# One array shape for a recommendation tower: sums and full-width steps in array tiles of 64 rows by 32 columns, one bank of sums per target, chunks of 64 steps

## What is computed

```python
e = jnp.stack([tbl_0[ids[:, 0]], ..., tbl_31[ids[:, 31]]], axis=1)        # 2048 x 32 x 64
z = jnp.sum(e, axis=-1)
outer = jnp.einsum('bpd,pde,bpe->bp', e[:, II, :], kernels, e[:, JJ, :])  # 496 pairs
h = jnp.concatenate([z, outer, dense_ctx], axis=1)                        # 544 wide
h = jnp.maximum(h @ W_top1 + b_top1, 0.0)                                 # 512
h = jnp.maximum(h @ W_top2 + b_top2, 0.0)                                 # 256
y = h @ W_top3
```

## Time and profile before

| | |
|---|---|
| median of 3 runs | 868.84 us (868.46 to 869.98) |
| the profiled execution | 869.06 us, span 867.2 us |
| PE busy, matmul records | 842.1 us (97%), 6584 |
| PE weight loads, records | 403.7 us, 6584 |
| DVE busy | 622.6 us (72%) |
| POOL busy | 483.9 us (56%) |
| ACT busy | 151.9 us (18%) |
| granted TensorE clock | 1.00 throughout |

### The profile page before, as it was taken

One profiled execution on the slowest core, in us unless ns is written; L12 is line 12 of the kernel. 1 busy time (PEld: TensorE's weight loads), 2 busy tenths in 40 slices (PEclk: granted clock), 3 DMA queues, 4 the chain that ended last, 5 costly groups with the idle time before them and its releaser, 6 DMA issues.

```text
span 867.2 us, 15755 instructions
## 1 busy us (share of the span) xinstructions
PE 842.1 (97%) x6584; PEld 403.7 (47%) x6584; DVE 622.6 (72%) x706; ACT 151.9 (18%) x273; POOL 483.9 (56%) x518
## 2 busy tenths in 40 slices
PE   2999999999999999999999999999999999999998
PEld 1888888776645333333333333333333333333333
DVE  1776677688865888888855488888855678888850
ACT  1222312212311220120210320020111212011002
POOL 6765777777777777777776477667733430000000
PEclk9999999999999999999999999999999999999999
DMA  9511111111111111111111011111100000000000
GB/s 327 195 25 25 27 32 28 27 29 30 27 28 26 28 28 26 31 27 26 28 26 25 16 24 26 25 25 26 26 13 13 14 16 1 1 1 1 1 1 1
DMA packets 24353, 28.32 MB, mean 33 GB/s; under 512 B 13398, under 2 KB 13657, under 8 KB 24156
## 3 DMA queue, kind: packets, MB, share of 16 engines
q0 software_dynamic: 16384, 16.81, 9.8%
q1 hardware_dynamic: 7888, 10.49, 3.6%
q10 hardware_dynamic: 12, 0.01, 0.0%
HBM read 27.27 MB, written 0.01 MB: 31 GB/s over the span
## 4 chain that ended last, share of the span: by engine, by line
PE 95%; DVE 2%; DMA 1%; issue 1%; POOL 1%; ACT 0%; DVEq 0%; ACTq 0%
PE y L610 52%; PE acc L627 26%; PE y L657 5%; PE y L593 4%; PE y L685 3%; DVE prod L558 2%; PE y L668 2%; PE y L662 1%; PE y L698 1%; POOL rows L365 1%; DMA rows<-tbl,ids_sb 1%; PE y L639 0%; DMA ids_sb<-ids 0%; DVEq L259 0%; ACT h L478 0%
## 5 line engine op out<-in xcount | busy, mean ns | idle before, releaser
L558 DVE TENSOR_TENSOR prod<-y,xt 128x1024 f32<-128x1024 f32 (+2 forms) x600 | 581.8, 1031 | 198.3 <-PE y L610 197.3
L365 POOL DMA_INDIRECT rows<-tbl,ids_sb x512 | 483.2, 944 | 222.8 <-issue 112.1
L610 PE MATMUL y<-xt,kw 64*128 64x512 f32 (+2 forms) x2976 | 476.7, 462 | 4.7 <-DVE prod L558 3.5
L610 PEld LDWEIGHTS y<-xt,kw 64*128 64x128 f32 x2976 | 242.7, 189 | 219.3 <-issue 201.9
L627 PE MATMUL acc<-prod,ones_strip 128*32 128x512 f32 (+2 forms) x2976 | 239.4, 454 | 0.3 <-DVE prod L558 0.3
L627 PEld LDWEIGHTS acc<-prod,ones_strip 128*32 128x32 f32 x2976 | 79.4, 109 | 142.4 <-issue 68.1
L411 ACT COPY xt<-y 128x1024 f32<-128x1024 f32 (+3 forms) x56 | 36.2, 646 | 297.0 <-PE y L593 296.9
L593 PE MATMUL y<-ident,rows 128*128 128x128 f32 x256 | 41.2, 288 | 16.2 <-DMA rows<-tbl,ids_sb 16.1
L530 DVE TENSOR_REDUCE z_rows<-rows 128x8 f32<-128x512 f32 (+2 forms) x96 | 44.5, 497 | 15.0 <-DMA rows<-tbl,ids_sb 15.0
L442 ACT COPY h_in<-acc 128x512 f32<-128x512 f32 (+2 forms) x24 | 10.6, 443 | 240.4 <-PE acc L627 240.4
L593 PEld LDWEIGHTS y<-ident,rows 128*128 128x128 f32 x256 | 28.0, 142 | 40.8 <-issue 32.6
(11 more groups left out here) (23 smaller groups left out, 66.7 us busy)
## 6 DMA issues: line engine op xcount, KB each, us to landing
rows<-tbl,ids_sb POOLq DMA_INDIRECT x512, 2.4
kw<-pair_k SPq DMA_DIRECT2D x14, 512.0 KB, 11.4
w_sb<-w SPq DMA_DIRECT2D x1, 1024.0 KB
w_sb<-w SPq DMA_DIRECT2D x1, 512.0 KB
kw<-pair_k SPq DMA_DIRECT2D x1, 384.0 KB
kw<-pair_k SPq DMA_DIRECT2D x1, 256.0 KB, 3.9
w1z_sb<-w1z SPq DMA_DIRECT2D x1, 256.0 KB
ids_sb<-ids SPq DMA_DIRECT2D x1, 240.0 KB, 2.7
```

The source lines that it names most:

```text
L365: pool.indirect_dma_start(out=rows[:, s, c, h, :], out_offset=None, in_=tables[f], in_offset=bass.IndirectOffsetOnAxis(ap=ids_sb[:, b, f:f ...
L558: nc.vector.tensor_tensor(prod_part(t, d, n), y_part(t, d, n), x, ALU.mult).then_inc(y_read, n)
L610: last = nc.tensor.matmul(y[:, h, :], kw[part, d, :], xt[part, slot_of(t, units[h][0] // 2), 0:w], start=True, stop=True)
```

## The change

All sums, and the steps of the tiles of 512 samples, are issued in array tiles of 64 rows by 32 columns. There are eight such tiles in the array: two halves of the rows by four quadrants of the columns.

- A step at width 512 issues eight matmuls in place of two: four column quadrants by two row halves, each 64 rows by 32 columns by 512. Steps at widths 128 and 256 keep their 64x128 matmuls.
- Each unit's sum issues two matmuls in place of one: partitions 0 to 63 (target n = 0) into bank 0 of `accs`, partitions 64 to 127 (n = 1) into bank 1. `ones_strip` has ones in one column. A quadrant has 32 places, so that a chunk is 64 steps (CHUNKS goes from 4 to 2).
- `accs` is one buffer of two banks where two buffers of one bank alternated. A chunk's first sum waits for ACT's copy of the chunk just before. ACT copies 128 x 1024 values in one instruction, half as often.
- `mlp1` reads four pieces as before: two of them before the last `acc_read` wait and two behind it, where it was three and one. The weights w1 are laid out to match.

```diff
-STRIPS = 16
+STRIPS = 32
+SPLIT_WIDTH = 512
+def step_columns(t):
+    return 32 if WIDTHS[t] >= SPLIT_WIDTH else P
 ...
-        accs = [bank(f"acc{i}", [P, TILE]) for i in range(2)]
+        accs = bank("accs", [P, 2, TILE])
 ...
-                nc.scalar.copy(h_in[:, c, 0:w], accs[(CHUNKS * t + c) % 2][:, 0:w]).then_inc(acc_read, 1)
+                nc.scalar.copy(h_in[:, c, :, 0:w], accs[:, :, 0:w]).then_inc(acc_read, 1)
 ...
-                for h in range(2):
-                    part = slice(DIM * h, DIM * h + DIM)
-                    last = nc.tensor.matmul(y[:, h, :], kw[part, d, :], xt[part, slot_of(t, units[h][0] // 2), 0:w],
-                                            start=True, stop=True)
+                size = step_columns(t)
+                for first in range(0, P, size):
+                    columns = slice(first, first + size)
+                    for h in range(2):
+                        part = slice(DIM * h, DIM * h + DIM)
+                        last = nc.tensor.matmul(y[columns, h, :], kw[part, d, columns],
+                                                xt[part, slot_of(t, units[h][0] // 2), 0:w], start=True, stop=True)
 ...
-                if first % CHUNK_STEPS == 0 and c >= 2:
-                    pe.wait_ge(acc_read, c - 1)
+                if first % CHUNK_STEPS == 0 and c >= 1:
+                    pe.wait_ge(acc_read, c)
                 pe.wait_ge(y_read, N_STEPS * t + end)
                 for u in range(2 * first, 2 * end):
                     q, s = unit_place(u)
-                    last = nc.tensor.matmul(acc[32 * q:32 * q + 32, 0:w], ones_strip[:, 30 - 2 * s:62 - 2 * s],
-                                            prod_part(t, u // 2)[:, u % 2, :],
-                                            start=s == 0, stop=ends_chunk(t, g) and u >= 2 * end - QUADRANTS)
+                    for n in range(2):
+                        part = slice(DIM * n, DIM * n + DIM)
+                        last = nc.tensor.matmul(accs[32 * q:32 * q + 32, n, 0:w],
+                                                ones_strip[part, STRIPS - 1 - s:2 * STRIPS - 1 - s],
+                                                prod_part(t, u // 2)[part, u % 2, :], start=s == 0,
+                                                stop=ends_chunk(t, g) and u >= 2 * end - QUADRANTS)
```

More of the change, by code:

```diff
@@ L57 @@
 UNITS = 2 * N_STEPS
-CHUNKS = -(-N_STEPS // (2 * STRIPS))
 CHUNK_STEPS = 2 * STRIPS
+CHUNKS = -(-N_STEPS // CHUNK_STEPS)
 PAIRS = FIELDS * (FIELDS - 1) // 2
@@ L272, in tower_program @@
         rows = sb("rows", [P, GATHER_SLOTS, TILE // P, 2, DIM])
-        h_in = sb("h_in", [P, CHUNKS, TILE])
+        h_in = sb("h_in", [P, CHUNKS, 2, TILE])
         z_rows = sb("z_rows", [P, TILE // P, 2, DIM])
@@ L277, in tower_program @@
         h2 = sb("h2", [P, J2, TILE])
-        w1_sb = sb("w1_sb", [P, CHUNKS, N1])
+        w1_sb = sb("w1_sb", [P, CHUNKS, 2, N1])
         w1z_sb = sb("w1z_sb", [P, N1])
@@ L285, in tower_program @@
         ident = sb("ident", [P, P])
-        ones_strip = sb("ones_strip", [P, 62])
+        ones_strip = sb("ones_strip", [P, 63])
         y_banks = [bank(f"y{i}", [P, 2, TILE]) for i in range(Y_SLOTS)]
-        accs = [bank(f"acc{i}", [P, TILE]) for i in range(2)]
+        accs = bank("accs", [P, 2, TILE])
         first_ids_loaded = sem("first_ids_loaded")
@@ L517, in _ @@
             dve.wait_ge(strip_zeroed, 1)
-            dve.memset(ones_strip[0:DIM, 30:31], 1.0).then_inc(consts_made, 1)
-            dve.memset(ones_strip[DIM:P, 31:32], 1.0).then_inc(consts_made, 1)
+            dve.memset(ones_strip[:, STRIPS - 1:STRIPS], 1.0).then_inc(consts_made, 1)
             dve.wait_ge(z_rows_zeroed, 1)
@@ L617, in sum_group @@
                 c = CHUNKS * t + first // CHUNK_STEPS
-                acc = accs[c % 2]
                 w = WIDTHS[t]
-                if first % CHUNK_STEPS == 0 and c >= 2:
-                    pe.wait_ge(acc_read, c - 1)
+                if first % CHUNK_STEPS == 0 and c >= 1:
+                    pe.wait_ge(acc_read, c)
                 pe.wait_ge(y_read, N_STEPS * t + end)
@@ L656, in mlp1 @@
                     for c in range(CHUNKS - 1):
-                        nc.tensor.matmul(y[:, h, 0:w], w1_sb[:, c, j * P:(j + 1) * P], h_in[:, c, 0:w],
-                                         start=c == 0, stop=False)
+                        for n in range(2):
+                            nc.tensor.matmul(y[:, h, 0:w], w1_sb[:, c, n, j * P:(j + 1) * P], h_in[:, c, n, 0:w],
+                                             start=c == 0 and n == 0, stop=False)
                 for h in range(2):
@@ L667, in mlp1 @@
                     j = 2 * pair + h
-                    last = nc.tensor.matmul(y[:, h, 0:w], w1_sb[:, CHUNKS - 1, j * P:(j + 1) * P],
-                                            h_in[:, CHUNKS - 1, 0:w], start=False, stop=True)
+                    for n in range(2):
+                        last = nc.tensor.matmul(y[:, h, 0:w], w1_sb[:, CHUNKS - 1, n, j * P:(j + 1) * P],
+                                                h_in[:, CHUNKS - 1, n, 0:w], start=False, stop=n == 1)
                 last.then_inc(y_full, 1)
@@ L700, in mlp3 @@
                 last.then_inc(y_full, 1)
-            pe.wait_ge(consts_made, 3)
+            pe.wait_ge(consts_made, 2)
             for what, t, n in PLAN:
@@ L745 @@
     k = np.zeros((P, N_STEPS, P), pair_k.dtype)
-    w1 = np.zeros((CHUNKS, P, N1), w_top1.dtype)
+    w1 = np.zeros((CHUNKS, 2, P, N1), w_top1.dtype)
     for d, step in enumerate(STEPS):
@@ L753 @@
                 k[DIM * h:DIM * h + DIM, d, DIM * n:DIM * n + DIM] = pair_k[pair] if i < f else pair_k[pair].T
-                w1[u // (QUADRANTS * STRIPS), 32 * q + 2 * s + n] = w_top1[FIELDS + pair]
+                w1[u // (QUADRANTS * STRIPS), n, 32 * q + s] = w_top1[FIELDS + pair]
     w1z = np.zeros((P, N1), w_top1.dtype)
@@ L764 @@
         dram_in("pair_k", k.reshape(P, N_STEPS * P)),
-        dram_in("w1", w1.transpose(1, 0, 2)),
+        dram_in("w1", w1.transpose(2, 0, 1, 3)),
         dram_in("w1z", w1z),
```

## The result

The changed kernel takes 858.39 us (median of 4 runs, 857.99 to 859.74) against 868.92 us before (4 runs): a ratio of 0.988, 95% interval 0.987 to 0.990. It is 10.5 us faster, where 23.8 were forecast; 858 lies inside the range of 840 to 869, but less than half of the expected gain is there.

A forecast was written before the change was run, and what follows sets the result against it. PE bounds the kernel, busy 842.1 of 867.2 us. Borders 11.2 + 12.4 + 2.3, less stagger 2.0 and the end 0.1, make 23.8 us off 869.06: 845 us, range 840 to 869.

The forecast's parts named there:

- Sums of tiles 0 to 2: Sums beside 64x128 steps: twice the matmuls at width 128 cost 0, bounds 0 and 30 us; width 256 at the shown pace.
- rivals 2 and 3: Respectively: late loads at step 3's gate return part of the gain, 852 us, 0.13; borders still empty the array, 869, 0.07.
- Rival 1: Instruction supply too slow at step 3 and width-128 sums: 905 us at 31 ns a pair, break-even 20 ns; chance 0.13.
- the gate of step 3: Step 3 of each width-512 group waits for DVE's read, then 16 load-matmul pairs follow: 0.31 us late at 31 ns each.
- Borders at width 512: Equal shapes of steps and sums avoid emptying and exposed loads: 11.2 + 12.4 us, plus 2.3 us at blocks behind other work.
- Rivals 3 and 4: Respectively: borders still empty the array, 869 us, chance 0.07; eight parts do not run at once, over 1,300 us, 0.05.
- Eight parts at once, cost zero: Steps at width 512: eight matmuls in eight array parts still take two rounds per step, so no added time.
- Stagger: Last of eight parts starts 0.05 us after the first, not 0.02: 66 blocks before other work lose 0.03 each, 2.0 us.
- The wait on y_read: Step 3 of a width-512 group waits for DVE to free its buffer: margin 0.12 us, in time under 9 ns a pair.
- Rival 2: Step 3's last loads come late behind DVE, returning part of the gain: 852 us, covering 846 to 869; chance 0.13.
- One accumulator pair: Chunk's first sum and mlp1 wait for ACT's copy: hidden behind other work; uncovered, a copy would cost 1.1 us, 11 times.
- Gathers: POOL's gathers before 260 us: no cost expected; PE about 1 us earlier at the eighth couple, with 3 to spare.

The follow-up runs named there:

- steps_128: The changed kernel with the steps of all widths, 128 and 256 too, in array tiles of 64 rows by 32 columns: 913.76 us, ratio 1.052.
- wide_only_b: The changed kernel with the sums at width 128 in the old form (128 rows by 32 columns), on a later chip: 844.58 us, ratio 0.973.
- half_stream: The changed kernel with each sum matmul at width 128 streaming 64 samples instead of 128, same instructions and order: 854.98 us, ratio 0.984.
- after_again: The changed kernel, unaltered, timed again on a chip of the first kind: 1,273.74 us, ratio 1.099.

## Why the prediction was half wrong

*The step that failed* is "Sums of tiles 0 to 2", with its "I take 0, from the spacing in the round", and in it width 128. The bounds there, 0 and 30 us, held. Against 29.3 us in the kernel before, the sixteen blocks take 41.8: the term was 12.5 us, and with the old form put back 13.8 us go. The trace of the changed kernel divides it: seven stops at late blocks of instructions, 6.8 us, and 32 pauses of 0.11 to 0.24 us, 5.2 us; two of the pauses account for most of the step from 1.88 to 2.24 us. The first part is shown by its place and by the packets; for the second no cause is shown. The error was one of reading: neighbours 7 ns apart, four in a row, were taken as evidence for 128 in a row, and the prediction had no term for instructions that arrive in blocks. The same paragraph had the right test (128 pairs every 15 ns) and the only row on a lasting pace said 31.

That 858 lies in the range is luck: the range was opened for rivals 2 and 3, and neither came true.

*Rival 1*, the supply of instructions, had the place of that loss, and for 6.8 of its 12.5 us the cause. Its threshold of 20 ns was for the whole kernel. Its other half, the gate of step 3, costs 1.2 us at most, see below. The pace differs between a burst and a block: matmuls in the eight parts of the array start 7 ns apart in a burst (eight from 609.43 to 609.48 us), 64 of them follow each other at 13.6 ns (0.109 us a round), and behind these most starts in the block at 64.66 us are 16 or 17 ns apart. The seven stops are late instruction packets, of 16,384 bytes and 256 of PE's instructions each. In steps_128, where packets are late, one comes per 3.83 us; in wide_only_b 256 instructions last 6.5 to 6.9 us in tile 0, and there is no such stop. That some 3.8 us are enough is the author's estimate from the first of these.

*Borders at width 512* (11.2 + 12.4 + 2.3 us): right, with period, loads and blocks behind other work as computed; the runs with one half of the change add that the whole gain hangs on equal shapes. No row of the kernel before has a border between equal shapes; that it would cost nothing was the author's estimate, from the loads within a block. What the traces measure at the old borders is 0.12 and 0.21 us; that the array empties there is not shown. Rivals 3 and 4 are out.

*Eight parts at once, cost zero*: right at width 512, a round takes 0.43 us as before. *Stagger*: 0.03 us a block at width 256 (1.86 to 1.89), nothing on most sums before other work; the term was a little too large.

*The wait on y_read*: right. The sixteen loads pass in 0.22 us, and of 93 step blocks nine take 0.07 to 0.18 us over the 3.43 or 3.46 of the others, 1.2 us in all. Rival 2 is out: it was a burst here, so the 7 ns were the right number in this place.

*One accumulator pair*: right, PE has no idle time on ACT's copies; `mlp1` takes what it took, 8.32 us for each half at width 512 in both. *DVE*: 4.62 us and 0.54 idle, to the hundredth. *Gathers* cost nothing: the first steps began 0.3 us later in this execution, but the first sum 0.7 us earlier.

*Still open:* what differs on the first two chips. The profile shows nothing waited for in the stops there either, but they do not lie where a block of instructions ends. Kernels with finer instructions lose most, but the loss does not follow the count of PE's records: steps alone 11,048 records and 3%, sums alone 9,560 and 7%. On the later chips no such stops were seen, so no run isolates it. Open too are the small pauses in the sums at width 128.

## What to carry to other kernels

Cutting matmuls into array tiles of one shape removed the border between two kinds of work here (0.34 us a period) where all of it was cut alike, and added nothing to a round at width 512 (0.43 us in both). Each cut doubles or quadruples instructions, so do it by width: here it gained where a pair of load and matmul lasts 54 ns (width 512), broke even at 27 ns (256) and lost at 14 ns (128). Read the instruction queue's packets as you read any other transfer. By the late packets of steps_128, one per 3.83 us, 256 instructions or 128 pairs had to last some 3.8 us in this kernel, an estimate; at 54 ns a pair they take 6.9, at 27 ns 3.5. And number the engine's instructions: the 32 long stops of steps_128, all at instruction 193 or 194 of 256, were late packets, and that place told the same of the changed kernel's seven. Last, compare on the chip you will run on: the ratio of this change was 0.988 on one and 1.099 on another.

## What the runs showed of the hardware

- Pace of load and matmul to eight array tiles of 64 rows by 32 columns. In the changed kernel the eight matmuls of a round at width 512 start 7 ns apart (from 609.43 to 609.48 us), and the sixteen loads of a step 3 pass in 0.22 us (row at 609.37). At width 128 the block of 128 pairs at 64.66 us takes 2.24 us, 17.5 ns a pair, with pauses of 0.14 and 0.21 us inside; in half_stream, with 64 samples, the block at 63.70 us takes 1.90 us, 14.8 ns a pair, with pauses of 0.21 and 0.29 us.
- Instruction packets. The changed kernel has 28,654 PE records for 112 packets of 16,384 bytes, the kernel before 13,785 for 54: 256 to a packet. In steps_128 34 packets start from 31.20 to 157.68 us, one per 3.83 us.
- Time of a packet. In the changed kernel's trace a packet's transfer takes 0.88 to 1.46 us (median 1.02). In the traces of the later chips PE never went on with its instructions less than 2.15 us after its start (the lowest, in steps_128); in the changed kernel's trace the lowest is 2.24 us. In steps_128 the next packet mostly started 1.0 to 1.4 us (at times up to 1.9) after PE had gone on.
- Rounds at width 512. Eight array tiles of 64 rows by 32 columns stream 512 fp32 values at once in 0.43 us a round (the changed kernel, 609.43 to 609.86 us). The kernel before has 0.43 us with two tiles of 64 by 128 (432.13 to 432.56 us) and with four of 128 by 32 (430.20 to 430.63 us).
- Chips. The kernel before took 868.5 to 868.9 us on some chips, at a granted clock of 1.00, and 1,149 and 1,158 us on two others, at 0.90 to 0.92. The trace of the changed kernel on one of these two (after_again) has loads of PE about 0.7 and 1.4 us apart, the granted clock at 0.92 over the span, and 201 us at the lower level, 0.5, all before 488 us. Of its stops over 0.5 us in mid-sum, one in 161 lay at instruction 193 or 194 of 256; on the first run's chip it was six of seven, and the seventh waited for DVE at the kernel's end.
